# Mixture-of-experts stage of a fused hybrid kernel: the down products in three runs instead of eight, and the gate chain in one piece

## The reference, cut to what matters

```
logits = flat @ router_w.T
probs = softmax(logits)
topk_probs, topk_idx = top_k(probs, 2)
topk_probs = topk_probs / (sum(topk_probs) + 1e-09)
gates = einsum('nk,nke->ne', topk_probs, one_hot(topk_idx, 8))
h1 = einsum('nc,ehc->neh', flat, w1)
h3 = einsum('nc,ehc->neh', flat, w3)
h = silu(h1) * h3                       # 682 hidden rows for each expert
y = einsum('neh,ech->nec', h, w2)
out = einsum('ne,nec->nc', gates, y)
```

## Time and profile before

| | before |
|---|---|
| median of 3 runs | 200.75 us (200.68 to 201.4) |
| profiled execution, span | 199.8 us |
| PE busy | 189.0 us, 95% |
| DVE busy | 154.2 us, 77% |
| ACT busy | 138.2 us, 69% |
| granted TensorE clock | full in all 40 slices |

### The profile page before, as it was taken

How to read it: one execution, slowest core, us unless ns; L and a number is a source line. 1 busy time by engine, 2 the same in 40 slices (tenths; PEclk the granted TensorE clock), 3 DMA queues, 4 the chain that set the end, 5 groups by cost and what they waited for, 6 DMA issues and landing times.

```text
span 199.8 us, 2692 instructions
## 1 busy us (share of the span) xinstructions
PE 189.0 (95%) x771; PEld 86.9 (43%) x773; DVE 154.2 (77%) x257; ACT 138.2 (69%) x286; POOL 101.5 (51%) x121
## 2 busy tenths in 40 slices
PE   7799999799999998999899999989999999999993
PEld 2334654344545534455345455836333333233231
DVE  6486899999999999999989954757676553945652
ACT  2629896999999999989989914555853452443430
POOL 7676668698899859999799900000000224000000
PEclk9999999999999999999999999999999999999999
DMA  4699543437958669683967200000000443000000
GB/s 148 143 240 176 167 159 110 144 125 219 270 187 215 185 170 289 226 211 118 310 205 234 73 0 0 3 0 0 0 0 7 126 102 74 17 3 0 0 0 26
DMA packets 20941, 23.38 MB, mean 117 GB/s; under 512 B 7897, under 2 KB 12478, under 8 KB 20926
## 3 DMA queue, kind: packets, MB, share of 16 engines
q1 hardware_dynamic: 20750, 23.11, 41.0%
q10 hardware_dynamic: 176, 0.10, 0.2%
HBM read 22.92 MB, written 0.28 MB: 116 GB/s over the span
## 4 chain that ended last, share of the span: by engine, by line
PE 48%; DMA 12%; DVE 7%; POOL 5%; issue 5%; SPq 0%; DVEq 0%; POOLq 0%
PE ps L1204 20%; PE ps L1224 10%; PE ps L986 8%; DMA cr<-c_rows 6%; DMA c_rows<-cb 6%; POOL rings L439 5%; DVE rings L717 4%; PE ps L993 2%; PE ps L909 1%; DVE ps L707 1%; PE ps L1154 1%; PE ps L1234 1%; PE ps L1173 1%; PE ps L1262 1%; PE ps L1074 1%
## 5 line engine op out<-in xcount | busy, mean ns | idle before, releaser
L439 POOL TENSOR_TENSOR rings<-rings,cr 128x512 f32<-128x512 f32 x59 | 73.4, 1270 | 10.4 <-DVE rings L717 4.7
L717 DVE TENSOR_TENSOR_SCAN rings<-rings,ps 128x512 f32<-128x512 f32 x64 | 74.3, 1200 | 0.6 <-ACT rings L536 0.4
L613 ACT ACTIVATE si<-ps 128x512 f32<-128x512 f32 (+1 forms) x44 | 26.3, 597 | 31.2 <-PE ps L1204 30.8
L886 DVE TENSOR_TENSOR rings<-ps,si 128x512 f32<-128x512 f32 (+1 forms) x42 | 28.8, 689 | 23.8 <-ACT si L613 23.3
L536 ACT ACTIVATE rings<-delta,a_neg 128x510 f32<-128x510 f32 x64 | 43.5, 707 | 0.0
L1204 PE MATMUL ps<-fd,wup 64*128 64x512 f32 (+1 forms) x136 | 41.3, 606 | 0.6 <-DVE fd L819 0.5
L517 ACT ACTIVATE scaled<-du_tok,b_tok 128x128 f32<-128x128 f32 x116 | 36.7, 387 | 0.7 <-PE ps L993 0.6
L986 PE MATMUL ps<-rings,ident 128*128 128x512 f32 x64 | 33.1, 599 | 1.8 <-POOL rings L439 1.8
L986 PE MATMUL ps<-rings,flip 128*128 128x512 f32 x64 | 32.3, 598 | 0.7 <-POOL rings L439 0.7
L461 POOL TENSOR_TENSOR fdg<-fd,gb 64x512 f32<-64x512 f32 x4 | 5.0, 1268 | 49.7 <-DMA gb<-g_rows 49.7
L1204 PEld LDWEIGHTS ps<-fd,wup 64*128 64x128 f32 (+1 forms) x136 | 15.7, 182 | 23.7 <-issue 12.4
(11 more groups left out here) (215 smaller groups left out, 179.2 us busy)
## 6 DMA issues: line engine op xcount, KB each, us to landing
cr<-c_rows SPq DMA_DIRECT2D x60, 256.0 KB, 3.8
wup<-w_up_dram SPq DMA_DIRECT2D x8, 341.0 KB, 5.8
wdn<-w_down_dram SPq DMA_DIRECT2D x4, 160.0 KB
wdn<-w_down_dram SPq DMA_DIRECT2D x4, 128.0 KB
gb<-g_rows SPq DMA_DIRECT2D x4, 128.0 KB, 4.7
delta<-g_rows SPq DMA_DIRECT2D x4, 128.0 KB, 3.7
w_conv<-conv_w_dram SPq DMA_DIRECT2D x1, 384.0 KB, 4.8
gmap<-g_rows SPq DMA_DIRECT2D x2, 172.0 KB
```

The source lines that it names most:

```text
L439: nc.gpsimd.tensor_tensor(hc[:, q], hs[:, q], cr[:, row_slot(n)] if n >= ROWS_FROM else cs[:, q], ALU.mult).then_inc(weighted, 1)
L613: nc.scalar.activation(si[0:rows, S % 2, :], ps[0:rows, BANK_H + 2 * (S % 3), :], ACT.Silu).then_inc(silu_ready, 1)
L717: nc.vector.tensor_tensor_scan(hs[:, q, :], da[:, q].rearrange("p b l -> p (b l)"), driven(q), 0.0, ALU.mult, ALU.add).then_inc(scanned, 1)
L886: nc.vector.tensor_tensor(gated[0:rows, S % GATED, :], linear, si[0:rows, S % 2, :], ALU.mult).then_inc(glu_ready, 1)
```

## The change

The down products go in three runs: set 0 whole behind step 10, set 1 whole behind step 21, and sets 2 and 3 behind step 43. To hold the tiles that long, the gated tiles get 22 slots, 16 in `rings` as before and 6 in `cr`, a buffer that the scan stage no longer needs. The gate chain stands in one piece behind glu(10), and ACT's exponential and its table loads behind the SiLU of step 10. `gate_pair(0)` and `gate_pair(1)` stand together behind glu(21); before they stood behind glu(24) and glu(27).

```
-GATED = 4 * BODY
+GATED = 2 * STEPS
+        def gated(S):
+            slot = S % GATED
+            return ringed[:, slot] if slot < 4 * BODY else cr[:, slot - 4 * BODY]
...
-                    if S == 7:
+                    if S == STEPS - 1:
                         nc.scalar.preload_act_table_set("exp_and_others")
...
-                    gate_step(S)
-                    if pair == PAIRS - FOLDED and s in (2, 5):
-                        gate_pair(s // 3)
+                    if S == STEPS - 1:
+                        gates()
+                if pair == PAIRS - FOLDED - 1:
+                    for gated_pair in range(PAIRS - FOLDED):
+                        gate_pair(gated_pair)
...
-                    if pair and s == 1:
-                        for j in range(GROUPS // 2, GROUPS - int(pair > PAIRS - FOLDED)):
-                            downs(pair - 1, j)
...
-                    if s == 7:
-                        for j in range(GROUPS // 2):
-                            downs(pair, j)
-            for j in range(GROUPS // 2, GROUPS - 1):
-                downs(PAIRS - 1, j)
+                if pair < PAIRS - FOLDED:
+                    for j in range(GROUPS):
+                        downs(pair, j)
+            for pair in range(PAIRS - FOLDED, PAIRS):
+                for j in range(GROUPS - 1):
+                    downs(pair, j)
             shared_downs()
```

More of the change, by code:

```diff
@@ L125, in hybrid_kernel @@
         hs, cs, hc = (rings[:, r].rearrange("p (q t) -> p q t", q=BODY) for r in (1, 2, 3))
-        gated = rings[:].rearrange("p r (q t) -> p (r q) t", q=BODY)
+        ringed = rings[:].rearrange("p r (q t) -> p (r q) t", q=BODY)
         b_tok = sb("b_tok", [P, NT, 2, 2 * N])
@@ L833, in softmax @@
                 chain(nc.vector.tensor_tensor(pb[:], le[:], over(g3[:], E), ALU.mult))
[L835 to L860, removed]
@@ new lines, in gates @@
+            def gates():
+                softmax()
+                chain(nc.vector.tensor_reduce(m1[:], pb[:], AX.X, ALU.max))
+                chain(nc.vector.tensor_tensor(key[:], pb[:], over(m1[:], E), ALU.is_equal))
+                chain(nc.vector.tensor_tensor(key[:], key[:], ranks, ALU.mult))
+                chain(nc.vector.tensor_reduce(g1[:], key[:], AX.X, ALU.max))
+                chain(nc.vector.tensor_tensor(oh1[:], key[:], over(g1[:], E), ALU.is_equal))
+                chain(nc.vector.scalar_tensor_tensor(pb2[:], oh1[:], -4.0, pb[:], ALU.mult, ALU.add))
+                chain(nc.vector.tensor_reduce(m2[:], pb2[:], AX.X, ALU.max))
+                chain(nc.vector.tensor_tensor(key[:], pb2[:], over(m2[:], E), ALU.is_equal))
+                chain(nc.vector.tensor_tensor(key[:], key[:], ranks, ALU.mult))
+                chain(nc.vector.tensor_reduce(g1[:], key[:], AX.X, ALU.max))
+                chain(nc.vector.tensor_tensor(oh2[:], key[:], over(g1[:], E), ALU.is_equal))
+                chain(nc.vector.tensor_tensor(oh1[:], oh1[:], oh2[:], ALU.add))
+                chain(nc.vector.tensor_tensor(g2[:], m1[:], m2[:], ALU.add))
+                chain(nc.vector.tensor_scalar(g2[:], g2[:], 1e-9, None, ALU.add))
+                chain(nc.vector.reciprocal(g3[:], g2[:]))
+                chain(nc.vector.tensor_tensor(pb[:], pb[:], over(g3[:], E), ALU.mult))
+                nc.vector.tensor_tensor(gate[:], oh1[:], pb[:], ALU.mult).then_inc(gate_ready, 1)
+                dve.wait_ge(gate_ready, 1)
@@ L885, in _ @@
                         dve.wait_ge(down_done, groups_through(S - GATED))
-                    nc.vector.tensor_tensor(gated[0:rows, S % GATED, :], linear, si[0:rows, S % 2, :], ALU.mult).then_inc(glu_ready, 1)
+                    nc.vector.tensor_tensor(gated(S)[0:rows], linear, si[0:rows, S % 2, :], ALU.mult).then_inc(glu_ready, 1)
                     if S == 2:
                         router_max()
-                    gate_step(S)
-                    if pair == PAIRS - FOLDED and s in (2, 5):
-                        gate_pair(s // 3)
+                    if S == STEPS - 1:
[3 more added lines that the diff above has]
+                        gate_pair(gated_pair)
             dve.wait_ge(y_gated, 3)
@@ L1224, in downs @@
                     last = nc.tensor.matmul(ps[e * C:(e + 1) * C, bank, :], wdn[0:rows, pair, tile, :],
-                                            gated[0:rows, (STEPS * pair + s) % GATED, :], start=first,
+                                            gated(STEPS * pair + s)[0:rows], start=first,
                                             stop=j == GROUPS - 1)
@@ L1234, in shared_downs @@
                     last = nc.tensor.matmul(ps[f * C:(f + 1) * C, BANK_O, :], wdn[:, pair, SHARED, :],
-                                            gated[:, (STEPS * pair + STEPS - 1) % GATED, :], start=False, stop=True)
+                                            gated(STEPS * pair + STEPS - 1), start=False, stop=True)
                 last.then_inc(down_done, 1)
```

## The result

The changed kernel takes 204.69 us (median of 4 runs, 204.06 to 207.16). The kernel before took 200.72 in the same set of runs. The ratio is 1.0188, 95% interval 1.0149 to 1.0228, so it is slower by 1.9%. I had forecast 201.4 us in a range of 198.6 to 202.6. The longest of the four, 207.16 us, had a mean granted clock of 0.982, the other three 0.990 to 0.992.

The account below looks back on a forecast made before the run. PE was taken as the bound, its order being the time in the expert stage. The terms, -1.90 - 0.54 + 2.65 + 0.43 = +0.64 us, take the median from 200.75 to 201.4 us, range 198.6 to 202.6.

Parts of the forecast that it names:

- term 1: Runs of downs on PE: eight become three, five fewer at 0.38 us each, 1.9 us saved.
- term 2: Old PE stalls in steps 8 to 12 (0.23 us) and 24 to 29 (0.31 us) go: 0.54 us saved.
- term 3: Gate chain in one piece behind glu(10): costs nothing, hidden by run 0 with 0.4 us of cover.
- term 6: `mixed` at step 32 delays glu(32), so PE stalls at step 35: 0.43 us lost with restart.
- term 5: gate_pair(1) waits for the half_in[1] transfer ahead of glu(22), so PE stalls at step 25: 2.65 us lost.
- term 7: No cost from the 22 slots, `cr` tiles, `fdg` transfers of set 3, `mixed` at step 43 or the last glu.
- Term 4: Transpose of the gates comes 0.6 us earlier, `gT` is kept at 152.48, and SP's later DMAs land 0.6 us earlier.
- rival C: PE's clock falls in the stall to 1.2 GHz, 0.855 us more per step: 202.3 to 204.8 us; chance 0.06.
- A: The forecast itself: the stall at step 25, transfer queue unchanged; 201.4 us, itself 200.7 to 202.0; chance 0.60.
- B: half_in[1] has landed when run 1 ends, so no stall at step 25: 198.7 us; chance 0.14.
- D: The 0.38 us belongs to the number of down groups, not runs: 203.3 us, half true 202.3; chance 0.10.
- E: Transfers land 0.5 to 1.5 us later than counted: 201.9 to 202.9 us; chance 0.10.

Follow-up runs that it names:

- Version 2: The changed kernel with only gate_pair(1) moved, to behind glu(43), beside the last run of downs: 198.35 us, 0.9886 of before; repeated, 198.54 us.
- experiment 8: Version 2 with eight of the ten down groups of sets 2 and 3 standing alone between steps, eight more runs: 200.78 us, 0.9991 of before.
- run 0: Not a follow-up kernel: the changed kernel's first run of down products on PE, set 0 whole behind step 10, six groups, measured at 5.30 us.
- experiment 9: Version 2 with the gate chain in six pieces and ACT's exponential in their old places: 201.7 us, 1.0037 of before.
- experiment 10: Version 2 with the five down groups of set 2 in a run of their own behind step 34: 198.69 us, 0.9898 of before.
- Experiment 3: The changed kernel with 17 products of zeros on PE behind step 24, inside its idle: 203.04 us, 1.0092 of before.
- Experiment 4: The changed kernel with GpSimd's two fdg products of set 3 held until both gate pairs are through: 204.41 us, 1.0149 of before.
- experiment 6: The changed kernel with SP issuing both half_in pairs directly behind the first two gb transfers: 199.05 us, 0.9868 of before.
- experiment 7: The kernel before, its eight runs kept, with both gate pairs moved behind glu(21): 207.33 us, 1.0275 of before.
- run 1: Not a follow-up kernel: the changed kernel's second run of down products on PE, set 1 whole behind step 21, forecast at 5.30 us.

## Why the prediction was wrong

**Terms 1, 2, 3 and 6 were right.** They add up to -1.90 - 0.54 + 0 + 0.43 = -2.01 us. Version 2 has these parts of the change and not term 5, and its stage is 59.54 against 61.56: -2.02 us. That the sum agrees to 0.01 us is in part luck: term 2 compares the steps 8 to 12, which stand behind a run of downs, with steps behind the transpose (4.49 us), while five steps behind a run take 4.56 us at 159.72 and at 175.40 of the chain before; by these it is 0.07 smaller. The price of a run, 0.38, measured 0.37 (experiment 8). The chain of gates was covered by run 0 (it ended at 149.9, the first glu behind it waited for its SiLU), and without that arrangement 2.5 us are lost (experiment 9). The stall of `mixed` is real: in version 2 step 35 starts 0.28 us late and its first half step is 0.11 longer, 0.39 us where 0.43 was said (experiment 10 takes it away). One small thing was missed, in term 7: the shared downs take 0.88 us in the chain and not 1.10. Before, the last glu ended at 194.51, only 0.06 us ahead of them, so it had most likely just held them up; no run separates this. These 0.2 us lie outside the stage lengths.

**Term 4 was right**: the gates are in `gT` at 152.17, forecast 152.48, in an execution whose expert stage began 0.33 us earlier.

**Term 5 is the step that failed, in its size.** Its place, kind and releaser are as forecast: VectorE behind a transfer into `delta`, PE idle at step 25. It said "2.65 us lost"; the runs say 65.59 - 59.54 = 6.05 us, with version 2 as the kernel without the wait. The step took the wait as the whole price, at the operation times and the landing of a kernel in which VectorE does not wait. The difference has three parts.

- The clock, 1.7 us. I had it as rival C with a chance of 0.06, and took the stall as harmless in the sum. Experiment 3 shows the price: fill the idle and 1.65 us are gone, with the wait still there. What was wrong was to give it so small a chance when no row showed an idle of such length, and when the forecast itself made one. The Trainium skill (TensorE: Matmul & The Clock Gate, Why this matters for your kernels) warns of idle gaps between bursts; I had cited it and then weighted it by the rows of a kernel that has no such gap. The trace agrees: the granted clock halved after or in each of the three idles of 3.05 to 4.08 us.
- The addition in `gate_pair(1)`, 1.0 us. I took its 0.69 us from a place where GpSimd was idle, and did not see that the stalled `gate_pair(1)` would start when `gate_in[1]` had just landed too, so just when GpSimd works on `fdg`. The addition began at 168.47, GpSimd's second product ran until 169.61, and the glu behind the addition started at 170.08. Experiment 4 removes the neighbour and has 0.69 us. The multiplication ahead of it, with one operand in PSUM, kept its 0.69 us beside GpSimd. The Trainium skill (SBUF — State Buffer, Who interferes with whom) has just this rule: a VectorE instruction with two inputs in SBUF contends with a GpSimd instruction that reads SBUF. The trace agrees: 1.69 us beside, 0.69 us alone.
- The landing, 0.6 us. From the copy of `gT` it took 167.72 - 152.17 = 15.55 us and not 14.96, in which 0.4 us lie in the issue that the queue held up (3.68 us at 157.18, 3.27 before) and 0.2 in the transfer itself (5.50 us, not 5.3). Step 22 and the copy of `gT` both came 0.3 us earlier than forecast, which leaves the wait as it is. In the other profiles in which VectorE waited it was 15.1 to 15.9 us. I had taken one value from one execution, though I had named the spread.

2.65 + 1.70 + 1.00 + 0.59 is 5.94; about 0.1 us of the 6.05 remains unassigned.

**The rivals.** A was right as a mechanism, too small as a size. B was wrong for this kernel, but experiment 6 shows its mechanism: with the transfer earlier, the change gives what B promised, 0.987 of before (I had 198.7 of 200.75, 0.990). C happened, on top of A as it was priced, and its sign came too: a slice behind 167 with a lower clock. By its own count the 1.70 us are two steps, which gives 201.4 + 2 x 0.855 = 203.1; that the measured 204.69 lies in its interval, 202.3 to 204.8, is luck, since the other 1.6 us come from the addition and the landing. D is out by experiment 8. E happened too, with 0.1 to 0.9 us on the landing.

## What to carry to other kernels

When a change moves an operation that waits for a transfer ahead of the work that feeds the bound engine, the wait is only the first price. Ask what the waiting operation will run beside when it is released, because the same event may release its neighbour, and what the bound engine's clock does in the idle, because that cost comes on top and need not shrink with the gap (experiment 4). And put such an operation where its engine is idle anyway: here one line moved to the end turned +1.9% into -1.2%.

## What the runs showed of the hardware

- A shorter idle of PE can cost more clock. After 4.08 us idle the granted clock was at half for about 3.4 us, 1.70 us lost. After 3.30 us idle it was at half for about 7 us, 3.0 us lost; there it had fallen inside the idle, at about 168.7, and in the first case only behind it, at about 172. After 3.05 us (experiment 7) it fell about at the restart, and the mean clock of single executions of that kernel lay between 0.992 and 0.98. The trace doesn't say what decides between them. An idle of 2.21 us (experiment 9) left the clock full in its profile.
- By these rows the addition beside GpSimd was not slowed but held. In three profiles (after, experiments 3 and 7) it took 1.69, 1.51 and 1.56 us, and GpSimd's second product ended 1.14, 0.95 and 1.01 us behind its start: each time that rest and 0.55 us, within 0.01. The page's spans on GpSimd are rough, so the 0.55 is less sure than the pattern. GpSimd's two products took 2.48 to 2.51 us with the addition beside them or without.
- In profiles with a full clock the expert stage repeats to 0.01 us (61.56 and 61.55 for the kernel before; 59.54 twice for version 2), while its start moved between 131.6 and 134.8 us. So between these profiles the time differs by the stages ahead.
- The down products that read tiles in `cr` cost the same as those in `rings`: in version 2 run 1, with seven of its twelve products on `cr`, takes 5.31 us, and run 0, all on `rings`, 5.31 as well.
